# Layer 1, self-attention: VectorE subtracts a pair's maxima, ScalarE takes all its exps in one instruction, VectorE sums the rows

## The reference

```python
def _fq(x, delta, zp, n_bits):
    xi = _round_ste(x / delta) + zp
    xq = jnp.clip(xi, 0.0, 2.0 ** n_bits - 1.0)
    return (xq - zp) * delta

def _attn(x, ctx, wq, wk, wv, wo, bo, dq, dk, dv, dw):
    ...
    sim = jnp.einsum('bhid,bhjd->bhij', _fq(q, dq, 128.0, 8), _fq(k, dk, 128.0, 8)) * SCALE
    attn = jax.nn.softmax(sim, axis=-1)
    out = jnp.einsum('bhij,bhjd->bhid', _fq(attn, dw, 0.0, 8), _fq(v, dv, 128.0, 8))
    ...
h1 = _ln(x, ln1_g, ln1_b)
x = _attn(h1, h1, a1_wq, a1_wk, a1_wv, a1_wo, a1_bo, d_q1, d_k1, d_v1, d_w1) + x
h2 = _ln(x, ln2_g, ln2_b)
x = _attn(h2, context, a2_wq, a2_wk, a2_wv, a2_wo, a2_bo, d_q2, d_k2, d_v2, d_w2) + x
h3 = _ln(x, ln3_g, ln3_b)
hg = h3 @ ff_w1 + ff_b1
a, g = jnp.split(hg, 2, axis=-1)
x = a * jax.nn.gelu(g, approximate=False) @ ff_w2 + ff_b2 + x
```

## Time and profile before

| | us |
|---|---|
| median of three runs | 4802.89 |
| lowest, highest | 4801.43, 4808.14 |
| the profiled execution | 4812.69 |
| its span | 4810.9 |

### The profile page before, as it was taken

How to read it: one execution, slowest core, us unless ns; L and a number is a source line. 1 busy time by engine, 2 the same in 40 slices (tenths; PEclk the granted TensorE clock), 3 DMA queues, 4 the chain that set the end, 5 groups by cost and what they waited for, 6 DMA issues and landing times.

```text
span 4810.9 us, 83209 instructions
## 1 busy us (share of the span) xinstructions
PE 4351.9 (90%) x28960; PEld 3061.3 (64%) x28960; DVE 3218.1 (67%) x6578; ACT 2875.4 (60%) x8857; POOL 2645.9 (55%) x4388
## 2 busy tenths in 40 slices
PE   7999999776868686889999999999999999999998
PEld 4545455455656565656666666666667778777777
DVE  6877777566565656566666666666666676666665
ACT  5777667788888888883333333333344666666664
POOL 6878778666565656563444444444454444444443
PEclk9999999888889888989999999999999999999999
DMA  6666666533333233234333333333432000000000
GB/s 153 126 124 132 130 115 125 115 63 59 63 60 65 59 65 59 65 81 87 84 74 74 79 74 72 80 74 72 81 77 61 19 22 19 15 22 19 15 18 7
...
## 3 DMA queue, kind: packets, MB, share of 16 engines
...
...
## 4 chain that ended last, share of the span: by engine, by line
PE 66%; POOL 14%; ACT 7%; issue 6%; DMA 4%; DVE 4%; SPq 0%; POOLq 0%; ACTq 0%; DVEq 0%
PE ring L1446 46%; PE score L1375 7%; POOL e L1974 7%; ACT e L1575 4%; PE ring L1389 4%; POOL halves L1957 4%; PE ring L1427 3%; DMA probs<-halves 2%; PE ring L1435 2%; DMA planes<-halves 1%; POOL e L1971 1%; PE ring L1386 1%; PE ring L1410 1%; DVE nmax L1710 1%; DVE probs L1745 1%
## 5 line engine op out<-in xcount | busy, mean ns | idle before, releaser
L1974 POOL TENSOR_SCALAR e<-e,rsum 112x375 f32<-112x375 f32 (+1 forms) x2048 | 1197.5, 601 | 1273.0 <-DVE rsum L1717 1239.8
L1575 ACT ACTIVATE e<-score,nmax 112x375 f32<-112x375 f32 (+1 forms) x2048 | 1036.8, 533 | 389.7 <-DVE nmax L1710 388.3
L1710 DVE TENSOR_REDUCE nmax<-score 112x2 f32<-112x750 f32 (+1 forms) x1152 | 1072.5, 949 | 286.2 <-PE score L1375 283.2
L1446 PE MATMUL ring<-h,weights 128*128 128x224 f32 x3840 | 896.4, 374 | 42.1 <-ACT work L1636 24.0
L1446 PEld LDWEIGHTS ring<-h,weights 128*128 128x128 f32 x3840 | 738.3, 199 | 201.1 <-issue 92.3
L1375 PE MATMUL score<-keys,q 64*112 64x375 f32 (+2 forms) x3584 | 642.9, 502 | 234.0 <-ACT e L1575 229.1
L1446 PE MATMUL ring<-weights,ctx 128*128 128x512 f32 (+4 forms) x1536 | 586.8, 515 | 0.0
L1745 DVE COPY probs<-planes 128x1344 uint16<-128x1344 uint16 x512 | 480.9, 940 | 151.4 <-DMA planes<-halves 146.2
L1375 PEld LDWEIGHTS score<-keys,q 64*112 64x112 f32 (+2 forms) x3584 | 223.1, 166 | 555.5 <-ACT e L1575 318.0
L1446 PE MATMUL ring<-ctx,weights 128*128 128x375 f32 x1536 | 568.3, 492 | 0.9 <-DVE heads L1810 0.7
L1575 ACT ACTIVATE e<-score,nmaxc,quant 112x375 f32<-112x375 f32 (+1 forms) x1024 | 554.5, 554 | 10.7
(11 more groups left out here) (128 smaller groups left out, 5789.4 us busy)
## 6 DMA issues: line engine op xcount, KB each, us to landing
ctx<-ctx_t SPq DMA_DIRECT2D x128, 375.0 KB, 3.3
...
probs<-halves SPq DMA_TRANSPOSE x320, 2.7
...
```

The source lines that it names most:

```text
L1446: ins = pe.matmul(out_, a, b_, start=n == 0, stop=n == len(parts) - 1)
L1575: ins = nc.scalar.activation(e_of(u)[:, n * width:(n + 1) * width], score_bank(u)[0:S, n * width:(n + 1) * width], ACT.Exp, bias=minus, sc ...
L1710: ins = dve.tensor_reduce(to, src, AX, ALU.max, negate=True)
L1974: ins = nc.gpsimd.tensor_scalar(mine, mine, rsum[0:S, slot(u), n:n + 1], 0.0, ALU.mult, ALU.add)
```

## The change

For the self pairs of layer 1 the chain between maxima and inverted sums is another. VectorE adds the negated maxima to the scores, reading PSUM and writing `e` (kind "lower", one TENSOR_TENSOR over 112x896). ScalarE takes one exp over the 896 elements in SBUF, in place, with the quantiser's factor as its scale, without bias and without an accumulated output; the scaling of the maxima is gone. VectorE sums each row of 112 (kind "sum", one TENSOR_REDUCE). TensorE's later scores wait for the subtraction where they waited for the exps. The wait for a free slot of `e` moves from ScalarE to VectorE. The planner's cost of the rounding becomes 0.7 and 0.6 where it was 1.0 and 0.85, for self and cross pairs. The scheduler then arranges layer 1 anew; layer 0 up to its last stream and the products of layers 2 and 3 keep their order.

```diff
--- before.py
+++ after.py
@@ -41,6 +41,7 @@
 TURN_LAG = 2.2
 QUADS = (2, 3)
 PV_BY = ("V", "VA", "V", "V")
+LOWER = (1,)
 AHEAD = 6.0
 TABLES = "natural_log_exp_and_others"
@@ -255,6 +256,13 @@
         at = self.nth_halved[p] % SPLITS * 4 * CHUNKS * P
         return at, at + 4 * CHUNKS * P
+    def lowered(self, p):
+        return p.octet.layer in LOWER and p.octet.attn == "self"
+
+    def scores_read(self, p):
+
+        return ("lower" if self.lowered(p) else "exp"), p
+
     def in_words(self, o):
         return o.layer in WORDS and o.attn == "cross"
@@ -420,7 +428,12 @@
             if self.lead(p) is p:
                 self.add("scores", p, "T", scores * (1.1 if o_.layer in (1, 3) and o_.layer in QUADS else 2 if o_.layer in QUADS else 1), p.index)
             self.add("max", p, "V", 1.12 if own else 0.96, p.index + 0.3)
-            self.add("exp", p, "A", (3.5 if own else 1.32) + (0.32 if q else 0), p.index + 0.5)
+            if self.lowered(p):
+                self.add("lower", p, "V", 1.05, p.index + 0.4)
+                self.add("exp", p, "A", 1.0, p.index + 0.5)
+                self.add("sum", p, "V", 1.0, p.index + 0.8)
+            else:
+                self.add("exp", p, "A", (3.5 if own else 1.32) + (0.32 if q else 0), p.index + 0.5)
             self.add("invert", p, "V", 0.17, p.index + 0.9)
             self.add("weigh", p, "G", (2.7 if own else 1.15) + (0.3 if q else 0), p.index + 1.0)
             if self.in_words(o_):
@@ -431,7 +444,7 @@
                 self.add("flip", p, "D", 3.5, p.index + 1.6)
                 self.add("merge", p, MERGE_BY, 0.9 if MERGE_BY == "V" else 1.2, p.index + 2.4)
             if q:
-                self.add("eight", p, "V", 1.0 if own else 0.85, p.index + 1.6)
+                self.add("eight", p, "V", 0.7 if own else 0.6, p.index + 1.6)
                 self.add("flip", p, "D", 2.5, p.index + 1.8)
         for j in self.jobs:
             self.add("job", j, "T", self.tensor_cost(j), j.pos)
@@ -502,12 +515,16 @@
                 yield "scores", self.lead(self.pairs[p.index - 1])
             for i in (1, 2) if o.layer in QUADS else (2,):
                 if p.index >= i:
-                    yield "exp", self.pairs[p.index - i]
+                    yield self.scores_read(self.pairs[p.index - i])
             for j in self.query_jobs(o) + self.key_jobs(o):
                 yield self.ready(j)
         elif kind == "max":
             yield "scores", self.lead(x)
-        elif kind == "exp":
+        elif kind == "exp" and self.lowered(x):
+            yield "lower", x
+        elif kind == "sum":
+            yield "exp", x
+        elif kind in ("exp", "lower"):
             yield "max", x
             if x.index >= ES // 2:
                 if self.pairs[x.index - ES // 2].octet.layer == 1:
@@ -541,7 +558,7 @@
             for o in self.probs_before(x.octet):
                 yield "job", self.pv_of[o]
         elif kind == "invert":
-            yield "exp", x
+            yield ("sum" if self.lowered(x) else "exp"), x
         elif kind == "weigh":
             yield "invert", x
         elif kind == "job":
@@ -996,6 +1013,8 @@
         scored = sem("scored")
         maxed = sem("maxed")
         expd = sem("expd")
+        lowered = sem("lowered")
+        summed = sem("summed")
         inverted = sem("inverted")
         weighed = sem("weighed")
         stepped = sem("stepped")
@@ -1270,7 +1289,7 @@
         every, nth = plan.every, plan.nth
         eight_bit = {}
         for kind, by in (("exp", "A"), ("weigh", "G")):
-            ps = [x_ for k_, x_ in plan.order[by] if k_ == kind and x_.octet.layer == 1]
+            ps = [x_ for k_, x_ in plan.order[by] if k_ == kind and x_.octet.layer == 1 and not (kind == "exp" and plan.lowered(x_))]
             eight_bit.update({(kind, p): i + 1 for i, p in enumerate(ps)})
         def eight_bit_nth(p, kind):
@@ -1324,6 +1343,23 @@
         def weights_at(wait, layer, name):
             wait.wait_ge(weights_loaded[part_of(layer, name)], 16)
+
+        def scores_read(wait, p):
+            if plan.lowered(p):
+                wait.wait_ge(lowered, nth["lower", p])
+            else:
+                wait.wait_ge(expd, nth["exp", p])
+
+        def exps_free(wait, p):
+
+            if p.index >= ES // 2:
+                before = plan.pairs[p.index - ES // 2]
+                if before.octet.layer == 1:
+                    wait.wait_ge(stepped, nth["eight", before])
+                elif plan.in_words(before.octet):
+                    split_done(wait, before)
+                else:
+                    wait.done([plan.turn_of[u] for u in before.units])
         def flip_done(wait, p):
             n = nth["flip", p] - 1
@@ -1358,8 +1394,8 @@
             if layer in QUADS:
                 ps = [p, plan.pairs[p.index + 1]]
             if p.index >= 2:
-                wait.wait_ge(expd, max(nth["exp", plan.pairs[p.index - 1 - i]] for i in range(2)
-                                       if i or layer in QUADS))
+                for before in plan.pairs[p.index - 2:p.index if layer in QUADS else p.index - 1]:
+                    scores_read(wait, before)
             wait.products(plan.query_jobs(o))
             wait.products(plan.key_jobs(o))
             masked = is_own(o) and layer == 3
@@ -1554,15 +1590,13 @@
         def scalar_exp(wait, p):
             o = p.octet
+            if plan.lowered(p):
+                wait.wait_ge(lowered, nth["lower", p])
+                mine = e[0:S, pair_slots(p), :]
+                nc.scalar.activation(mine, mine, ACT.Exp, scale=quant[0:S, 4:5] if o.layer == 1 else 1.0).then_inc(expd, 1)
+                return
             wait.wait_ge(maxed, nth["max", p])
-            if p.index >= ES // 2:
-                before = plan.pairs[p.index - ES // 2]
-                if before.octet.layer == 1:
-                    wait.wait_ge(stepped, nth["eight", before])
-                elif plan.in_words(before.octet):
-                    split_done(wait, before)
-                else:
-                    wait.done([plan.turn_of[u] for u in before.units])
+            exps_free(wait, p)
             a = 0 if is_own(o) else 8
             width = width_of(o)
             if o.layer == 1:
@@ -1709,10 +1743,27 @@
                     to = nmax[0:S, pair_slots(p), 0:nt]
                     ins = dve.tensor_reduce(to, src, AX, ALU.max, negate=True)
                     ins.then_inc(maxed, 1)
+                elif kind == "lower":
+                    p = x_
+                    wait.wait_ge(maxed, nth["max", p])
+                    exps_free(wait, p)
+                    first = p.units[0].index % 4
+                    src = score[0:S, first:first + 2, 0:4 * S].rearrange("p a (i n) -> p a i n", i=4)
+                    top = nmax[0:S, pair_slots(p), 0:4].unsqueeze(3).to_broadcast([S, 2, 4, S])
+                    to = e[0:S, pair_slots(p), :].rearrange("p a (i n) -> p a i n", i=4)
+                    dve.tensor_tensor(to, src, top, ALU.add).then_inc(lowered, 1)
+                elif kind == "sum":
+                    p = x_
+                    wait.wait_ge(expd, nth["exp", p])
+                    src = e[0:S, pair_slots(p), :].rearrange("p a (i n) -> p a i n", i=4)
+                    dve.tensor_reduce(sums[0:S, pair_slots(p), 0:4], src, AX, ALU.add).then_inc(summed, 1)
                 elif kind == "invert":
                     p, o = x_, x_.octet
                     nt = count_of(o)
-                    wait.wait_ge(expd, nth["exp", p])
+                    if plan.lowered(p):
+                        wait.wait_ge(summed, nth["sum", p])
+                    else:
+                        wait.wait_ge(expd, nth["exp", p])
                     to = rsum[0:S, pair_slots(p), 0:nt]
                     ins = dve.reciprocal(to, sums[0:S, pair_slots(p), 0:nt])
                     ins.then_inc(inverted, 1)
```

## The result

The changed kernel takes **4769.7 us** (five runs, 4762.0 to 4778.0) where the kernel before took 4806.9 in the runs beside it (4801.4 to 4809.2): a ratio of 0.9925, 95% interval 0.9913 to 0.9937. That is 37 us faster, one third of the 112 us forecast. The sign was right and the time lies inside the range of 4630 to 4775 us, near its top; the forecast's own size was wrong.

The account below looks back on a forecast made before the run. ScalarE was taken to set part A and TensorE part B. Gains of 1.5 and 6.1 us, taken as 7.5 per period over 15 periods, took 112 us off 4802.9: 4691 us, range 4630 to 4775.

Parts of the forecast that it names:

- TensorE's 60 us per period: Layer 1, one period per stream of two batches: TensorE stays busy 60 us, less if its clock rises.
- The step that moves six gate products and one key product: Layer 1: these products move from TensorE's full part into its idle one, saving 6.1 us per period.
- part B: Rest of a period outside part A, 44.9 us before, set by TensorE; forecast to lose 6.1 us.
- part A: From the first self pair's maxima to the end of the fourth's rounding; forecast 33.1 us, some 1.5 us gained.
- Part A has room: TensorE idles 16 us in it: Claim that the 6.1 us of products moved out of part B fit into TensorE's idle time in part A.
- S1 to S3: From the first self pair's maxima to the third's: the chain runs without large gaps, about 18.4 us.
- S3's sum some 5 us behind its maxima: Third self pair: its exp waits behind a gate product's save on ScalarE, putting its sum some 5 us late.
- The 2 us for "its exp and sum": Fourth self pair, end of part A: exp and sum take 2 us after maxima and subtraction, before GpSimd's weighing.
- The slower rival: VectorE stalls in part A as before: part A 42.4 us, run 15 us slower, 4818 us; chance 0.08.
- Rival "the gate save holds S3's exp": Part A stays or grows some 4 us, part B alone pays: 2 us per period, 4773 us; chance 0.18.
- The rival "TensorE is filled": Part A falls to 30.3 us, part B sheds 8 by a higher clock: 184 us, 4619 us; chance 0.06.
- The passes don't block GpSimd: Answers the rival that VectorE's new passes hold up GpSimd's weighing: 3.5 us per period left, 4751 us; chance 0.05.

Follow-up runs that it names:

- e5: The changed kernel with each self pair's exp (ScalarE) and sum (VectorE) moved up to two places ahead of saves and clips (the hoist): 4716.9 us.
- e13: The changed kernel with only the fourth self pair's sum moved ahead of the gate save just before it on VectorE: 4744.8 us.
- e15: The changed kernel with the first up save put ahead of the fourth self pair's rounding on VectorE: 4753.4 us.
- e16: e5 with each sum over only 14 of 112 columns of a row, so wrong values: 4715.4 us.
- e4: The changed kernel with each sum over only 14 of 112 columns of a row, so wrong values: 4690.7 us.
- e7: The changed kernel with three extra TensorE products ahead of each layer 1 attention-times-values group, as filler for its waits: 4774.0 us.

## Why the prediction was wrong

- **The removed and added work: right.** ScalarE's exp took 1.03 us (0.94 taken), so a pair sheds 2.7 us instead of 2.8. The estimate from the Trainium skill (ScalarE: Activation LUTs, What ACT_TABLE_LOAD costs), 1.03 us, was the better one; the line through two other forms was 9% low. The passes took 1.09 and 1.08 us (1.08 taken). Per period ScalarE came to 59.1 us (59) and VectorE to 54.6 (55).
- **The wait removed: right.** TensorE's wait for the exps went from 14.1 to 5.4 us per period ("under 6").
- **TensorE's 60 us per period: wrong.** It took 65.3. The step that moves six gate products and one key product, priced at full speed, charged the moved work at part B's clock, and credited part B alone. Part B shed 8.5 us, more than the 6.1 forecast, since more moved than I counted (70 matmul records, where my six gate products are 24). But its work landed in a part A at 0.76 of the clock and took 12.8 us there, where 7.9 left part B. "Part A has room: TensorE idles 16 us in it" was the error: the room is made of waits, and a product that is made slowly delays the save behind it, and that save's queue.
- **Part A's 33.1 us: the step that failed.** It took 41.6, past the 41 at which I called myself wrong. S1 to S3 took 21.9 us (18.4 forecast, "without large gaps"), and from S3 on 19.7 (14.7 forecast). In the first, VectorE waits 2.3 us per period for the late exps of S1 and S2. In the second, two terms failed:
  - "S3's sum some 5 us behind its maxima": it starts 7.5 us behind (mean of eleven periods). I counted the gate save ahead of S3's exp on ScalarE and not the one ahead of S3's sum on VectorE, which waits 3.4 us per period for its product; in e5, where that exp is done 3.3 us behind the maxima, the sum still starts at 6.7. And I priced the products in front of both saves at full speed, so the exp itself was done only at 6.9: the self heads' and the key product took 3.3 us in the period shown, not 1.7. The DMA that I gave 1.5 us was over 0.03 us behind S3's maxima, which took back part of it.
  - The 2 us for "its exp and sum" put the exp and the sum of S4 straight behind its subtraction, so that GpSimd would weigh S3 and S4 one behind the other. The order has five gate saves ahead of that exp and one ahead of that sum; the sum starts 4.7 us behind the maxima, and GpSimd stands idle 2.08 us between the two weighings.

  e5, which moves the four exps and S4's sum forward, brings part A back to 37.5 and the period down by 7.5 us from the kernel before, to 72.8. That this equals the forecast's 7.5 is chance: it is 2.3 us longer in A and 9.7 shorter in B.
- **The slower rival, 0.08, had part A's number, in part by luck.** It said that VectorE would idle 12.1 us there and that part A would be 42.4 us; it idled 41.63 - 29.98 = 11.7, and part A was 41.6. But it placed the idle time in the four sums and in front of the rounding. Those hold 2.3 and 2.2 us of it; 4.7 us are the two gate saves that wait for TensorE's product, which it didn't name. It took the shorter of two part A's, 34.4 us, as its base; from the mean, 35.2, its 7 us in part B would have cancelled the loss, and part B shed 8.5.
- **Rival "the gate save holds S3's exp"** named a right place (in the changed kernel S3's exp starts 5.9 us behind its maxima, with the hoist 2.2) and 4773 us, 3 us from the result. That nearness is luck: it had part A 4 us longer and part B 6.1 shorter, and they were 6.4 and 8.5. Its partner on VectorE, the gate save ahead of S3's sum, was missing here too.
- **A slip in a sum.** The rival "TensorE is filled" adds 34.4 - 30.3 = 4.1 and 8 to 12.3 us per period; it is 12.1, or 182 us. It changes nothing here.
- **The passes don't block GpSimd.** One of its 112x112 multiplies takes 392 ns on average where it took 389 before (1450 to 2000 us of both), and GpSimd is busy 46.6 us per period (48.3). This agrees with the lock's rule in the Trainium skill (SBUF — State Buffer, SBUF: two separate sides), by which these passes hold no lock.

So the missing 5.4 us per period (7.5 less 2.1) come from where exps, sums and saves stand in two in-order queues, and from what TensorE's slower products add. That order alone can bring as much back is shown by e5, and that a single place counts by e13 and e15; how the loss divides over S1 to S4 is read from one trace and not shown by a run for each. That VectorE's length isn't on the path in every order is shown by e16; in the changed kernel's own order it is (e4). What part the lower clock has of its own stays open: e5, e4 and e16 have shorter periods together with a higher clock, and the one run that raised it otherwise (e7) brought no time, but spent some on its filler and hardly raised part A's. Open too is why the up save ahead of the rounding gains 16 us in one order and costs 23 in the other.
